# Four gate products moved among the value projections in the inversion of a recurrent layer

## The reference

```python
q = silu(x @ Wq); k = l2norm(silu(x @ Wk)); v = silu(x @ Wv)
log_f = log_sigmoid(x @ Wf1 @ Wf2); beta = sigmoid(x @ Wbeta) * 2.0
# each token takes two steps; S is one 32 x 32 state for each batch and head
S = exp(g) * S + a_t * (b_t @ S) + k_t * v_t
o = q_t @ S
gate = x @ Wog1 @ Wog2                   # rank 32
y = rmsnorm(o * sigmoid(gate)) * norm_w
out = y @ Wo
```

## Time and profile before

| | us |
|---|---|
| three runs: lowest, median, highest | 1868.3, 1868.99, 1871.28 |
| the profiled execution: its time | 1866.4 |
| the profiled execution: its span | 1864.6 |
| busy: PE, DVE, ACT, POOL | 1578.4, 1124.8, 787.5, 767.4 |
| mean granted TensorE clock | 0.934 |

### The profile page before, as it was taken

How to read it: one execution, slowest core, us unless ns; L and a number is a source line. 1 busy time by engine, 2 the same in 40 slices (tenths; PEclk the granted TensorE clock), 3 DMA queues, 4 the chain that set the end, 5 groups by cost and what they waited for, 6 DMA issues and landing times. The chain is left out here.

```text
span 1864.6 us, 68387 instructions
## 1 busy us (share of the span) xinstructions
PE 1578.4 (85%) x26476; PEld 1282.4 (69%) x26477; DVE 1124.8 (60%) x3370; ACT 787.5 (42%) x1829; POOL 767.4 (41%) x986
## 2 busy tenths in 40 slices
PE   5499999999577879688896888967886999999994
PEld 5499999999435565355653556535564999999994
DVE  7646444444367885977859778588773546444441
ACT  2143333333277344673446734467332443333331
POOL 2554422222164661746617456164651234422221
PEclk9999999999889999788997889979897999999997
DMA  9563322232300200001000010000102743332324
GB/s 307 175 188 77 86 49 47 46 50 45 74 4 7 70 23 23 4 10 66 23 23 4 12 64 23 23 4 7 47 22 90 245 84 74 74 66 45 51 46 113
DMA packets 84240, 116.28 MB, mean 62 GB/s; under 512 B 12953, under 2 KB 74465, under 8 KB 82017
## 3 DMA queue, kind: packets, MB, share of 16 engines
q1 hardware_dynamic: 56160, 74.17, 13.0%
q0 software_dynamic: 27360, 37.80, 11.3%
q10 hardware_dynamic: 608, 2.96, 0.5%
HBM read 64.87 MB, written 54.21 MB: 64 GB/s over the span
## 5 line engine op out<-in xcount | busy, mean ns | idle before, releaser
L1067 POOL DMA_INDIRECT x<-ffn_yout,ffn_place x142 | 221.9, 1563 | 534.8 <-DVE ffn_yout L999 460.8
L1005 DVE TENSOR_TENSOR ffn_inner<-ffn_inner,ffn_bank 128x512 f32<-128x512 f32 x142 | 97.6, 687 | 340.0 <-PE ffn_bank L875 335.4
L875 PE MATMUL ffn_bank<-ffn_tileT,ffn_gate_now 128*128 128x128 f32 x2272 | 279.8, 277 | 0.0
L956 ACT ACTIVATE ffn_inner<-ffn_bank 128x512 f32<-128x512 f32 x142 | 84.8, 597 | 459.6 <-PE ffn_bank L875 459.6
L875 PE MATMUL ffn_bank<-ffn_tileT,ffn_up_now 128*128 128x128 f32 x2272 | 277.4, 275 | 0.0
L885 PE MATMUL ffn_bank<-ffn_w,ffn_inner 128*128 x1136 | 269.1, 380 | 2.2 <-DVE ffn_yout L999 2.0
L875 PEld LDWEIGHTS ffn_bank<-ffn_tileT,ffn_gate_now 128*128 128x128 f32 x2272 | 268.1, 194 | 0.1
L875 PEld LDWEIGHTS ffn_bank<-ffn_tileT,ffn_up_now 128*128 128x128 f32 x2272 | 265.7, 192 | 0.0
L885 PEld LDWEIGHTS ffn_bank<-ffn_w,ffn_inner 128*128 128x128 f32 x1136 | 205.0, 190 | 25.3 <-issue 3.3
L818 ACT COPY ffn_gate_now<-ffn_w 128x1024 f32 x142 | 148.4, 1045 | 29.8 <-issue 21.9
L818 DVE COPY ffn_up_now<-ffn_w 128x1024 f32 x142 | 99.3, 699 | 53.1 <-issue 42.0
(11 more groups left out here) (614 smaller groups left out, 3135.8 us busy)
## 6 DMA issues: line engine op xcount, KB each, us to landing
ffn_w<-in_w1t_dram SPq DMA_DIRECT2D x16, 1024.0 KB, 5.4
ffn_tile<-xs SPq DMA_DIRECT2D x122, 130.0 KB, 2.1
ffn_w<-in_w2t_dram SPq DMA_DIRECT2D x16, 512.0 KB, 6.7
at_a_sb<-x SPq DMA_DIRECT2D x32, 256.0 KB, 2.8
ffn_x<-in_x_dram SPq DMA_DIRECT2D x16, 256.0 KB, 5.2
x<-ffn_x SPq DMA_DIRECT2D x16, 256.0 KB, 5.2
x<-at_a_sb SPq DMA_DIRECT2D x16, 256.0 KB, 2.1
xs<-ffn_empty SPq DMA_DIRECT2D x23, 130.0 KB, 2.8
```

Source lines behind the costliest of these rows:

```text
L875: t = pe.matmul(bank[:, i * P:(i + 1) * P], half_now[half][b][:, k, i * P:(i + 1) * P], rowsT[b][:, k * P:(k + 1) * P], start=(k == 0), st ...
L956: act.activation(inner[b][:, :], p_g[b][:, :], ACT.Silu).then_inc(s_silu, 1)
L1005: dve.tensor_tensor(inner[b][:, :], inner[b][:, :], p_u[b][:, :], ALU.mult).then_inc(s_act, 1)
L1067: pool.indirect_dma_start(total, bass.IndirectOffsetOnAxis(ap=place[b][:, 0:1], axis=0), yout[b][:, :], None, compute_op=ALU.add).then_inc ...
```

## The change

`TURN` gives one order for the eight products on TensorE and the eight activations on ScalarE: values 0 and 1, gates 4 and 5, value 2, gates 6 and 7, value 3. All of them now stand between the 12th and 13th group of transposes. The gates' results go to banks 0 to 3, each after the key group that lay there is copied. The groups 12 to 15, which use these banks next, wait for the gates' tanh. `back(0)` to `back(3)` wait for all eight activations, and so does GpSimd before it prepares group 0 (it waited for the four values).

```diff
+    TURN = (0, 1, 4, 5, 2, 6, 7, 3)
...
-            pool.wait_ge(s_vale, 4)
+            pool.wait_ge(s_vale, TURN.index(3) + 1)
...
+                if KEYS <= n < KEYS + 4:
+                    pe.wait_ge(s_vale, TURN.index(n - KEYS + 4) + 1)
...
-                    pe.wait_ge(s_vale, 5 + n)
+                    pe.wait_ge(s_vale, 8)
...
             def gate(j):
                 t, g, c = VALUES[j]
-                pe.wait_ge(s_vale, j - 3)
-                pe.matmul(psum[j][:, :], wrank[RANK:2 * RANK, g * P:(g + 1) * P], fg[RANK:2 * RANK, c * 512:(c + 1) * 512],
+                pe.wait_ge(s_ev, KEYS - 7 + j)
+                pe.matmul(psum[j - 4][:, :], wrank[RANK:2 * RANK, g * P:(g + 1) * P], fg[RANK:2 * RANK, c * 512:(c + 1) * 512],
                           start=True, stop=True).then_inc(s_val, 1)
 
             for n in range(KEYS):
                 forth(n)
-            for j in range(4):
-                value(j)
+            for j in TURN:
+                if j < 4:
+                    value(j)
+                else:
+                    gate(j)
             for n in range(KEYS, GROUPS):
                 forth(n)
-            for j in range(4, 8):
-                gate(j)
```

More of the change, by code:

```diff
@@ L2501, in value @@
                 t, g, c = VALUES[j]
-                act.wait_ge(s_val, j + 1)
+                act.wait_ge(s_val, TURN.index(j) + 1)
                 act.activation(both(t, g, c), psum[4 + j][:, :], ACT.Silu).then_inc(s_vale, 1)
@@ L2506, in gate @@
                 t, g, c = VALUES[j]
-                act.wait_ge(s_val, j + 1)
-                act.activation(both(t, g, c), psum[j][:, :], ACT.Tanh, scale=0.5).then_inc(s_vale, 1)
+                act.wait_ge(s_val, TURN.index(j) + 1)
+                act.activation(both(t, g, c), psum[j - 4][:, :], ACT.Tanh, scale=0.5).then_inc(s_vale, 1)
             for n in range(KEYS):
```

## The result

The changed kernel took 1871.49 us (median of 22 runs, 1865.32 to 1875.23), the kernel before in the same comparison 1867.28 us (22 runs, 1859.89 to 1872.3). The ratio is 1.0021 with a 95% interval of [1.0011, 1.0030]: some 3.9 us slower. The forecast was 1866.2 us, with no time above 1870.8 in its range.

The account below looks back on a forecast made before the run. VectorE, which hardly stops, was taken to bound the four inversion blocks. Fewer clock-caused waits (-1.76 us) and shorter hold-ups by GpSimd (-1.0) gave -2.8 us, from 1868.99 to 1866.2 us; range 1862.0 to 1870.8.

Parts of the forecast that it names:

- It adds and removes no instruction: Premise for the whole change: it only moves four products and four tanh and rewires waits.
- The GpSimd rival: GpSimd's sends stay as long, group 1 is late, its preparation collides with the scan's first step: about 1872 us, chance 0.03.
- (a): VectorE's term 4, against groups complete at about 608.5 us: slack 1.4 us, cost nothing.
- (b): TensorE's sums: first starts at 608.5 us, second ends at 612.4, needed at 614.9; cover 2.5 us, cost nothing.
- the schedule: Values and gates in pass 0's times: activations end at 603.6 us, groups complete at about 608.5 instead of 604.9.
- the prediction's sign of being wrong: VectorE waits ahead of term 4, or a block exceeds 52 us with its clock low beyond 28 us.
- (c): TensorE's clock in the blocks: VectorE's waits for the sums go, -1.76 us, bounds 0 and 4.6 less.
- the thin stretch: TensorE, 604.7 to 608.5 us, only last two groups' transposes: clock falls behind it in some passes, at most 0.2 us.
- (e): GpSimd's preparation moves later and meets VectorE's smaller, last pairs: -1.0 us, bounds -2.35 and +2.1.
- The cover that the prediction named: At VectorE's last pairs TensorE is some 1.5 us behind VectorE, so part of the hold-up is hidden.
- (d): GpSimd's sends start at 608.7 us, last 22.8; group 1 stays in time, or 1.0 us late at the old length.
- nothing gained: Rival: the 1.76 us return as low clock at the sums, GpSimd holds up other pairs as long; 1869.0 us, chance 0.15.

Follow-up runs that it names:

- e10: The changed kernel with the copies' wait ahead of groups 12 to 15 replaced by four idle semaphore increments, against the kernel before: ratio 1.0014.
- e2: The changed kernel, unchanged, timed again against the kernel before: ratio 1.0021.
- e15: e6 with four idle TensorE increments in front of pass 1's first transposes, against the kernel before: ratio 1.0007.
- e1: The kernel before, unchanged, timed against itself as a measure of noise: ratio 0.9997.
- e4: The kernel before with GpSimd's sends made to wait for VectorE's term 3, as late as in the changed kernel: ratio 0.9998 of before.
- e5: The kernel before with one idle semaphore increment on TensorE ahead of each of groups 12 to 15, against the kernel before: ratio 0.9996.
- e7: The kernel before with five idle TensorE increments ahead of each of groups 12 to 15, 20 a pass, against the kernel before: ratio 1.0023.
- e13: e5 repeated unchanged, against the kernel before: ratio 1.0024.
- e14: The kernel before with four idle TensorE increments once, in front of pass 0's first transposes, against the kernel before: ratio 1.0023.
- e3: The changed kernel with four unread TensorE products added around the last two groups of transposes, against the kernel before: ratio 1.0034.
- e8: The changed kernel with GpSimd's sends started behind the last activation, its preparation still behind the last copy, against the kernel before: ratio 1.0010.
- e6: The changed kernel without TensorE's older wait on the copies ahead of groups 12 to 15, against the kernel before: ratio 0.9991.
- e11: e6 repeated unchanged, against the kernel before: ratio 0.9998.
- e12: e6 with four idle TensorE increments once, in front of pass 0's first transposes, against the kernel before: ratio 1.0017.

## Why the prediction was wrong

**The step that failed** is "It adds and removes no instruction". It has four more on TensorE in each pass, and they cost more than all terms of the sum together. The prediction read the change inside the block, where its four waits cost little (1.0021 with them, 1.0014 in e10 with four increments in their place), and nowhere else. No rival named the scan. The GpSimd rival's 1872 is near the measured time by luck: group 1, on which it rests, was not late. The profile before had the sign: 1.21 us of idleness inside a run of products that waits for no engine.

**(a), (b) and the schedule were right.** First sum at 22.3 us, forecast 21.6; sends from 22.5 us, forecast 21.8. Term 4 wasn't held up in passes 0 to 2 and by 0.20 us in pass 3, so the prediction's sign of being wrong came, at a size that hardly counts:

```profile
1318.61 1.76 DVE L2327 TENSOR_TENSOR end_a_top<-end_ng,at_tm 128x768 f32<-128x768 f32 x2 [0.20 <-ACT at_aq L2491]
```

**The clock (c).** It didn't fall among values and gates. In the profiled execution it didn't fall in the thin stretch, or at the sums behind it, either. Stretches of pass 0 after (us, each engine's busy time, TensorE clock, DMA), and the same thin stretch of pass 2:

```profile
600.00:606.00 6.00, 6.00 (x14) 2.21 (x13) 5.79 (x17) 4.25 (x8) 0.00 (x0) 1.00 0.00 0
606.00:611.70 5.70, 3.23 (x25) 2.74 (x23) 5.50 (x11) 5.03 (x15) 0.00 (x0) 1.00 0.02 4
611.80:616.00 4.20, 4.20 (x10) 1.92 (x11) 4.20 (x6) 2.82 (x2) 3.36 (x3) 1.00 0.16 57
```

```profile
1074.60:1080.30 5.70, 3.12 (x26) 2.74 (x24) 5.50 (x9) 5.17 (x16) 0.00 (x0) 1.00 0.00 0
```

5.7 us with hardly anything but transposes and idleness passed at 1.00 in all four passes. But one execution is not all. In e2, the same kernel, pass 0 ran through its thin stretch at 1.00 too and then had this:

```profile
612.30:615.70 3.40, 2.82 (x4) 1.26 (x5) 3.40 (x5) 3.37 (x4) 2.29 (x2) 0.50 0.11 39
```

Over the eleven traces with the new order the clock fell 21.5 to 24.3 us behind the first transpose, at the end of the thin stretch or just behind it, in 17 of 44 passes: for 3.4 us in 16 of them and 6.8 in one. So the forecast that it would fall there in some passes held, and so did the one that it would cost little. By the sentence of the Trainium skill on transposes that the prediction weighed (TensorE: Matmul & The Clock Gate, Part 4), the fall would be usual here; it came in fewer than half of the passes. With the old order it fell in 19 of 28, 17.9 to 21.9 us behind the first transpose and for up to 10.2 us.

VectorE's wait ahead of term 8 went as forecast, in all passes of the changed kernel's traces; of the other traces with the new order e10 had 0.88 us in one pass, behind its fall of 6.8 us, and e15 0.15. But the term was mis-sized: 1.76 us was what the profiled execution happened to have. In seven traces with the old order (before, e1, e4, e5, e7, e13, e14) these waits came to 3.15 us together, 0.45 in an execution. The single execution on which the sum was built was four times worse than the mean at this point.

The clock fell at a second place: in passes 2 and 3 the first key transposes of the changed kernel ran at the lower level.

```profile
1056.38 1.52 PE L2384 MATMUL at_bank<-at_consts,at_a_sb 128*128 128x128 f32 x8 [0.93 <-PEq L1299]
1057.69 1.92 PE L2384 MATMUL at_wide<-at_consts,at_a_sb 128*128 128x128 f32 x8
```

1.52 and 1.92 us, where pass 0 took 1.14 for the first; the 12th group is 1.6 us late by it. The clock was back at 1.00 from about 1060.4, while TensorE still ran nothing but transposes. That happened in 21 of 44 passes with the new order and in 6 of 28 with the old. Why is not settled: nothing in the block stands in front of it.

**(e) had the wrong sign.** I priced GpSimd's preparation at -1.0 us; the second half of VectorE's work and what follows it to the scan took 71.4 us in four passes (mean of after, e2, e3) against 69.6 (the seven old ones): +1.8 (e4, with its late sends, is one of the seven: 71.05). The cover that the prediction named, TensorE being 1.5 us behind VectorE, was not there at the 384-element pair. The trace of e8 shows it: with the sends started at 17.6 to 19.2 us instead of 22.5 to 24.1, the same stretch took 69.7. The ratio fell by 0.0011, 2 us, about what the hold-ups come to, but the two intervals overlap, and e4 had its longer stretch at 0.9998; so their price in time is read from the traces and not shown by the comparisons. The sends' end decides it finely: in e6, e10, e11, e12 and e15 they start as late as in the changed kernel, yet end sooner in some passes, and the stretch took 69.9. The sends' length, 22.6 us, was forecast well (22.8), so it was known when the preparation would come; only what it meets was misjudged. **(d)**'s lateness of group 1 didn't come: 0.32 us were left.

**The sum.** Forecast -1.76 - 1.0 = -2.8 us. By these traces: waits for the sums and ahead of term 4 -0.3, the pair +1.8, the transposes at the lower clock about +1.0 (an estimate: 7 of 12 passes of after, e2 and e3 against 6 of 28, each putting VectorE's second half some 0.7 us later), the scan of pass 0 +3.3; together +5.8 against 3.9 [2.1, 5.6] measured. The excess is a little more than the interval allows; the clock's part is the least certain of these, since single executions scatter by some us. The stretches between a scan and the next block also looked longer with the new order (340.5 us for three, mean of 11, against 338.8, mean of 7), with a scatter of 1 to 2 us each; whether that is real stays open.

Two numbers of the working are off by themselves. The top of the range is said to be nothing gained with the upper bound of (e), which gives 1869.0 + 2.1 = 1871.1 and not 1870.8; the 0.36 us for group 1 in that bound stands in no row. And the base, 1868.99, was the median of three runs, where the 22 runs have 1867.28.

## What to carry over

Count every instruction that a change adds to an engine, waits too, and look where its code meets the next loop: a wait that costs nothing where it stands can move a loop over an edge of the code, and a kernel with four idle instructions more shows the second stop in one trace (its time needed more than one comparison, as e5 and e13 tell). Before a stall of one profiled execution goes into the sum, look whether it recurs in the other passes, and weigh it by how often. A hold-up moved to a later place is hidden only if the engine behind it is shown to be late there.

## What the runs showed of the hardware that I had not expected

TensorE stands still where its code reaches an edge between two pieces of 256 instructions in the first turn of the scan's loop: for 0.6 to 2.2 us in pass 0 of these 18 traces, until 1.4 to 1.6 us behind the landing of a 16 KB transfer. Four instructions (e12, e14) decide whether there is one such stop in pass 0 or two. With the second, of some 1.6 us, the scan was about 3.3 us longer, since the clock also stayed low for 10 to 17 us instead of at most 7. TensorE's clock stayed at 1.00 through 5.7 us that held only transposes, with the array busy for 3.1 to 3.2 of them (passes 0 and 2 of the changed kernel), and in other executions fell to 0.50 right behind such a stretch.

VectorE's addition of two buffers took 1.86 us instead of 0.55 beside GpSimd's elementwise products. The Trainium skill (SBUF — State Buffer, section SBUF: two separate sides) describes a pair of ports of which one of the two engines has the use for a whole instruction while the other is fully blocked; the row agrees, with 1.3 us lost beside three products of GpSimd that took 0.84 and 0.42 us. Which of the two had the ports first the rows don't show: VectorE's addition is recorded from 634.55, GpSimd's first product from 634.78.
